# Attention projections as three products of rounded high and low parts, turned tokens in three buffers, the mask one batch at a time

## The reference

```python
src_trans = (src @ W_src.T + b_src) * mask[:, :, None]      # 256 x 512 per batch
tgt_trans = (tgt @ W_tgt.T + b_tgt) * mask[:, :, None]      # 256 x 256 per batch
k, v = split(src_trans); q = tgt_trans                      # 8 heads of 32
scores = where(mask == 0, -inf, q k^T / sqrt(32))
update = softmax(scores) @ v
x = x + tanh(g) * (concat([tgt, update]) @ W_out.T + b_out)
```

## Time and profile before

| | us |
|---|---|
| median of 3 runs | 698.89 |
| lowest, highest | 697.07, 701.77 |
| span of the profiled execution | 696.1 |
| PE busy | 657.9 (95%) |
| PE weight loads busy | 457.6 (66%) |
| ACT busy | 452.6 (65%) |
| DVE busy | 428.5 (62%) |
| POOL busy | 202.2 (29%) |

### The profile page before, as it was taken

How to read it: one execution, slowest core, us unless ns; L and a number is a source line. 1 busy time by engine, 2 the same in 40 slices (tenths; PEclk the granted TensorE clock), 3 DMA queues, 4 the chain that set the end, 5 groups by cost and what they waited for, 6 DMA issues and landing times.

```text
span 696.1 us, 11909 instructions
## 1 busy us (share of the span) xinstructions
PE 657.9 (95%) x3653; PEld 457.6 (66%) x3653; DVE 428.5 (62%) x981; ACT 452.6 (65%) x1204; POOL 202.2 (29%) x299
## 2 busy tenths in 40 slices
PE   5988899999999999699999999999999997799997
PEld 3754555554544447588888888888888875556654
DVE  7973857777765548466767566556665685343522
ACT  7766665535555534667887787788778877646452
POOL 6574424210110012124442342333223230142110
PEclk9999999999999999899999999999999999999999
DMA  8721108501000004433344443433444430001112
GB/s 269 244 96 61 62 31 257 81 1 61 1 0 1 0 1 124 101 87 99 98 113 123 123 116 84 107 93 94 119 122 122 92 80 14 2 1 61 43 49 90
DMA packets 45809, 57.90 MB, mean 83 GB/s; under 512 B 13152, under 2 KB 24258, under 8 KB 45634
## 3 DMA queue, kind: packets, MB, share of 16 engines
q1 hardware_dynamic: 45762, 57.33, 30.4%
HBM read 27.46 MB, written 4.19 MB: 45 GB/s over the span
## 4 chain that ended last, share of the span: by engine, by line
PE 79%; SPq 6%; DVE 3%; ACT 3%; DMA 3%; issue 2%; POOL 2%; DVEq 0%; POOLq 0%; ACTq 0%
PE bank L1197 12%; PE bank L1502 7%; PE bank L1414 6%; PE bank L1432 6%; PE bank L1209 6%; SPq L531 5%; PE bank L1455 5%; PE bank L1645 4%; PE bank L1478 4%; PE bank L1441 4%; PE bank L1495 4%; PE bank L1173 3%; PE bank L1635 3%; PE bank L1177 2%; PE bank L1636 2%
## 5 line engine op out<-in xcount | busy, mean ns | idle before, releaser
L976 ACT ACTIVATE c_junk<-bank,c_nmx 128x256 bf16<-128x256 f32 x256 | 116.6, 470 | 9.3 <-DVE c_nmx L1971 9.2
L1971 DVE TENSOR_REDUCE c_nmx<-bank 128x4 f32<-128x1024 f32 x64 | 75.3, 1219 | 35.7 <-PE bank L1455 35.7
L1197 PE MATMUL bank<-b_o,cw 128*128 128x512 f32 x192 | 90.6, 603 | 1.8 <-ACT b_o L831 1.8
L998 ACT ACTIVATE c_pT<-bank 128x1024 f32<-128x1024 f32 x64 | 62.0, 1017 | 7.0 <-PE bank L1478 5.9
L807 ACT ACTIVATE b_h<-bank,cb 128x512 f32<-128x512 f32 x48 | 32.9, 687 | 51.1 <-PE bank L1197 51.0
L1096 ACT ACTIVATE d_h<-bank,b_col 128x512 f32<-128x512 f32 x64 | 39.6, 686 | 39.3 <-PE bank L1636 39.3
L1197 PEld LDWEIGHTS bank<-b_o,cw 128*128 128x128 f32 x192 | 34.2, 190 | 43.4 <-issue 39.7
L1414 PE MATMUL bank<-c_ctxT,wsrcT 128*128 128x256 f32 x256 | 62.1, 388 | 0.6 <-ACT c_ctxT L957 0.6
L1432 PE MATMUL bank<-wsrcT,c_ctxT 128*128 128x256 f32 x240 | 56.7, 379 | 0.0
L1478 PE MATMUL bank<-c_stack 99*128 99x256 f32 x256 | 47.8, 320 | 7.9 <-DMA c_stack<-c_rows 7.5
L1414 PEld LDWEIGHTS bank<-c_ctxT,wsrcT 128*128 128x128 f32 x256 | 48.6, 194 | 7.2 <-ACT c_ctxT L957 0.9
(11 more groups left out here) (202 smaller groups left out, 1383.0 us busy)
## 6 DMA issues: line engine op xcount, KB each, us to landing
c_stack<-c_parts SPq DMA_DIRECT2D x192, 128.0 KB
a_ctx<-in_ctx SPq DMA_DIRECT2D x16, 512.0 KB, 4.0
c_ctx<-in_ctx SPq DMA_DIRECT2D x16, 512.0 KB, 3.3
out_x<-x_sb SPq DMA_DIRECT2D x7, 512.0 KB, 2.9
x_sb<-in_x SPq DMA_DIRECT2D x3, 1024.0 KB, 11.0
mask_b<-in_mask_BxS_fk SPq DMA_DIRECT2D x1, 2048.0 KB, 12.4
x_sb<-in_x SPq DMA_DIRECT2D x2, 512.0 KB, 5.6
wsrc_raw<-in_L_xattn_W_src SPq DMA_DIRECT2D x1, 1024.0 KB, 7.1
```

The source lines that it names most:

```text
L976: op = nc.scalar.activation(c_junk[:, tc, j, :], scores(tc)[:, j, :], ACT.Exp, bias=c_nmx[hg][:, tc, j:j + 1], accum_out=c_sum[hg][:, tc, ...
L998: nc.scalar.activation(c_pT[hg][:, :, q * S:(q + 1) * S], scores(q), ACT.Exp).then_inc(c_pT_ok, 1)
L1197: op = mm(bank[2 * u + h][:], cw1[:, c, h * P:(h + 1) * P], b_o[n % LANES][:, c, :], start=c == 0, stop=c == DK - 1)
L1971: v.tensor_reduce(c_nmx[hg][:, tc, :], scores(tc), AXIS.X, ALU.max, negate=True)\
```

## The change

Five things change. (1) Every projection of stage C becomes three float32r products, high by high, high by low and low by high, in one accumulation (in_parts, out_half). (2) For that each turned operand gets a low part: ACT's copy out of PSUM now writes the rounded high part, and DVE subtracts it from the PSUM bank (ctxL_c, xnL_c, updateL_c); PE's waits move from the copies to the low parts. The weights get theirs on POOL once (split_weights), from a full copy w_full. (3) The turned tokens are kept in three buffers (XNS), so that ACT's second copy goes; the first turn, xnT_c(0), moves into slot 11. (4) The mask is loaded per batch, 128 KB into one of two buffers (mask_in), and both uses of biased wait for it. (5) All 16 bodies are written out, without a loop. Some buffers are laid out anew in SBUF, and DVE's last xn_d(1) waits for the last token turn.

```diff
+XNS = 3
+PRODUCTS = ((0, 0), (0, 1), (1, 0))
...
-def over_batches(eng, body):
-
-    for b in range(HEAD):
-        body(b, b % 2)
-    with eng.Fori(HEAD // 2, B // 2 - 1) as i:
-        body(2 * i, 0)
-        body(2 * i + 1, 1)
-    for b in range(B - 2, B):
+def over_batches(body):
+
+    for b in range(B):
         body(b, b % 2)
...
-        mask_b = sb("mask_b", [P, B, S])
+        mask_b = [sb(f"mask_b{s}", [P, S]) for s in range(2)]
...
-        wsrcT = sb("wsrcT", [P, FK, 2 * D])
-        wtgtT = sb("wtgtT", [P, DK, D])
-        woutT = sb("woutT", [P, 2 * DK, D])
+        with ExitStack() as st:
+            w_full = sb("w_full", [P, 7, 512], F32, st)
+        wsrcT, wtgtT, woutT = zip(*([sb(f"{n}_{part}", [P, k, d], F32R)
+                                     for n, k, d in (("wsrcT", FK, 2 * D), ("wtgtT", DK, D), ("woutT", 2 * DK, D))]
+                                    for part in ("lo", "hi")))
+        wsrcT, wtgtT, woutT = wsrcT[::-1], wtgtT[::-1], woutT[::-1]
...
-            (mask_b[:], mask.partition_broadcast(P)),
...
+            def mask_in(b):
+                need(sp, c_q_ok, b - 1)
+                need(sp, c_k_ok, b - 1)
+                sp.dma_start(mask_b[b % 2][:], row_on_all(mask[b])).then_inc(c_mask_in[b % 2], 16)
+
+            mask_in(0)
+            mask_in(1)
...
                     masks_c(b + 1, 1 - b % 2)
+                if b + 2 < B:
+                    mask_in(b + 2)
                 if b + 3 < B:
                     stream_c(b + 3, 1 - b % 2)
...
+            def split_weights(t):
+                pool.wait_ge(s_wT, t + 1)
+                high, low = turned_rows(t)
+                nc.gpsimd.tensor_copy(high, w_full[:, t, :]).then_inc(s_wsplit, 1)
+                pool.wait_ge(s_wsplit, 2 * t + 1)
+                nc.gpsimd.tensor_tensor(low, w_full[:, t, :], high.bitcast(F32), ALU.subtract).then_inc(s_wsplit, 1)
+
+            for t in range(WT_BANKS):
+                split_weights(t)
...
-            def xnTq_c(b, src=5):
+            def xnT_c(b, src=5):
                 need(act, c_xnT_ps, b + 1)
-                need(act, c_q_ps, b)
-                need(act, c_xnT_ok, b)
-                nc.scalar.copy(c_xnTq[:].rearrange("p c t -> p (c t)"), bank[src][:]).then_inc(c_xnTq_ok, 1)
-
-            def xnT_c(b, s):
-                need(act, c_xnTq_ok, b + 1)
-                need(act, c_out_ps, b - 1)
-                nc.scalar.copy(c_xnT[s][:], c_xnTq[:]).then_inc(c_xnT_ok, 1)
+                need(act, c_out_ps, b - XNS + 1)
+                nc.scalar.copy(c_xnT[b % XNS][0][:].rearrange("p c t -> p (c t)"), bank[src][:]).then_inc(c_xnT_ok, 1)
...
-                xnT_c(b + 1, 1 - s)
                 if ahead:
-                    xnTq_c(b + 2)
+                    xnT_c(b + 2)
                 update_c(b, s, 0)
...
+            def in_parts(dst, still, moving):
+
+                chunks = len(still[0])
+                for i, (a, b) in enumerate(PRODUCTS):
+                    for f in range(chunks):
+                        op = mm(dst, still[a][f], moving[b][f], start=i == 0 and f == 0,
+                                stop=i == len(PRODUCTS) - 1 and f == chunks - 1)
+                return op
...
             def k_c(b, s, dst=4, parts=range(DK)):
-                need(pe, c_ctxT_ok, 2 * b + 2)
+                need(pe, c_ctxL_ok, 2 * b + 2)
+                turned = [[c[s][:, f, :] for f in range(FK)] for c in (c_ctxT, c_ctxL)]
                 for m in parts:
-                    for f in range(FK):
-                        op = mm(bank[dst][:, m * S:(m + 1) * S], wsrcT[:, f, m * P:(m + 1) * P],
-                                c_ctxT[s][:, f, :], start=f == 0, stop=f == FK - 1)
+                    weights = [[w[:, f, m * P:(m + 1) * P] for f in range(FK)] for w in wsrcT]
+                    op = in_parts(bank[dst][:, m * S:(m + 1) * S], weights, turned)
...
                 need(pe, c_xn_ok, b + 1)
-                need(pe, c_ctxT_ok, 2 * b + 1)
+                need(pe, c_ctxL_ok, 2 * b + 1)
...
             def q_c(b, s, dst=5):
-                need(pe, c_xnTq_ok, b + 1)
+                need(pe, c_xnL_ok, b + 1)
                 for m in range(DK):
-                    for c in range(DK):
-                        op = mm(bank[dst][:, m * S:(m + 1) * S], wtgtT[:, c, m * P:(m + 1) * P],
-                                c_xnTq[:, c, :], start=c == 0, stop=c == DK - 1)
+                    weights = [[w[:, c, m * P:(m + 1) * P] for c in range(DK)] for w in wtgtT]
+                    op = in_parts(bank[dst][:, m * S:(m + 1) * S], weights,
+                                  [[x[:, c, :] for c in range(DK)] for x in c_xnT[b % XNS]])
...
-                need(pe, c_up_ok, n - 1 if is_last(b, B) else n)
+                need(pe, c_upL_ok, n - 1 if is_last(b, B) else n)
...
-            def out_part(s, k, f):
-                src = c_xnT[s][:, f, :] if f < DK else c_upT[s][:, f - DK, :]
-                return mm(bank[7][:, k * D:(k + 1) * D], src[:, k * P:(k + 1) * P], woutT[:, f, :],
-                          start=f == 0, stop=f == 2 * DK - 1)
+            def out_half(b, s, k, h):
+
+                held = (c_xnT[b % XNS], (c_upT[s], c_upL[s]))[h]
+                dst = bank[7][:, k * D:(k + 1) * D]
+                for i, (p, q) in enumerate(PRODUCTS):
+                    for f in range(DK):
+                        op = mm(dst, held[p][:, f, k * P:(k + 1) * P], woutT[q][:, h * DK + f, :],
+                                start=h == 0 and i == 0 and f == 0,
+                                stop=h == 1 and i == len(PRODUCTS) - 1 and f == DK - 1)
+                return op
             def out_begin(b, s, k=0):
                 if k == 0:
-                    need(pe, c_xnT_ok, b + 1)
                     need(pe, c_x3, b)
-                for f in range(DK):
-                    out_part(s, k, f)
+                out_half(b, s, k, 0)
             def out_c(b, s, begun=(0,)):
-                need(pe, c_up_ok, 2 * b + 2)
+                need(pe, c_upL_ok, 2 * b + 2)
                 for k in range(TS):
-                    for f in range(DK if k in begun else 0, 2 * DK):
-                        op = out_part(s, k, f)
+                    if k not in begun:
+                        out_half(b, s, k, 0)
+                    op = out_half(b, s, k, 1)
...
             ctxT_c(0, 0, 1, 5)
             ctxT_c(0, 0, 0, 7)
-            xnT_c(0, 0, 6)
             slot_b(PAIRS - 1)
-            pe.wait_ge(c_ctxT_ok, 2)
+            pe.wait_ge(s_wsplit, 2 * WT_BANKS)
+            pe.wait_ge(c_ctxL_ok, 2)
             q_c(0, 0, 7)
             k_c(0, 0, 6)
             slot_b(PAIRS)
-            for k in range(TS):
-                for f in range(FK):
-                    op = mm(bank[3][:, k * D:(k + 1) * D], c_ctxT[0][:, f, k * P:(k + 1) * P],
-                            wsrcT[:, f, D:2 * D], start=f == 0, stop=f == FK - 1)
-            op.then_inc(c_v_ps, 1)
+            v_c(0, 0, 0, 3)
+            v_c(0, 0, 1, 3)
...
+                need(dve, c_mask_in[b % 2], 16 * (b // 2 + 1))
                 need(dve, ps, b + 1)
                 need(dve, used, use_count)
                 for m in range(DK):
                     op = v.scalar_tensor_tensor(dst[:, m, :], src_bank[:, m * S:(m + 1) * S], col[:, m:m + 1],
-                                                mask_b[:, bass.ds(b, 1), :].rearrange("p o t -> p (o t)"),
-                                                ALU.add, ALU.mult)
+                                                mask_b[b % 2][:], ALU.add, ALU.mult)
                 op.then_inc(ok, 1)
+
+            def ctxL_c(b, s, h, src=4):
+                need(dve, c_ctxT_ok, 2 * b + 2 - h)
+                need(dve, c_v_ps, b - 1)
+                v.tensor_tensor(c_ctxL[s][:, 2 * h:2 * h + 2, :].rearrange("p c t -> p (c t)"), bank[src + h][:],
+                                c_ctxT[s][:, 2 * h:2 * h + 2, :].rearrange("p c t -> p (c t)").bitcast(F32),
+                                ALU.subtract).then_inc(c_ctxL_ok, 1)
+
+            def xnL_c(b, src=5):
+                high, low = (part[:].rearrange("p c t -> p (c t)") for part in c_xnT[b % XNS])
+                need(dve, c_xnT_ok, b + 1)
+                v.tensor_tensor(low, bank[src][:], high.bitcast(F32), ALU.subtract).then_inc(c_xnL_ok, 1)
+
+            def updateL_c(b, s, hg):
+                need(dve, c_up_ok, 2 * b + hg + 1)
+                need(dve, c_out_ps, b - 1)
+                v.tensor_tensor(c_upL[s][:, hg, :], bank[6][:, hg * S:(hg + 1) * S],
+                                c_upT[s][:, hg, :].bitcast(F32), ALU.subtract).then_inc(c_upL_ok, 1)
...
             def last_c(b, s):
+                updateL_c(b - 1, 1 - s, 0)
                 maxima_c(b, s, 0)
                 xnT_d(1, 1)
                 xnT_d(1, 0)
                 shift_c(b, 0)
+                updateL_c(b - 1, 1 - s, 1)
                 maxima_c(b, s, 1)
                 finish_c(b - 1, 1 - s)
                 shift_c(b, 1)
```

(27 more changed lines are left out.)

83 lines of the change are left out of this document (50 added, 33 removed).

## The result

The changed kernel takes **739.9 us** (median of 4 runs, 735.9 to 742.7) against 698.0 for the kernel before on the same chip (4 runs, 696.1 to 701.8): 1.0587 times as long over all runs, with an interval of 1.054 to 1.063. The forecast was 708, with a range of 690 to 718. The direction was right, the size was not. The profiled execution has a span of 740.7 us against 696.1; it was the longest of the four (742.7, 2.7 above their median).

The account below looks back on a forecast made before the run. Relieved of PE's bound, the kernel was to be held by the loop through DVE and ACT with a late mask: +4.5, +2.7, +1.3, -0.5, +0.8 make +8.8, span 704.9, plus 2.8 for the median, 708 us; range 690 to 718.

Parts of the forecast that it names:

- PE's 95%: PE's busy share of the span before; PE may lose 2 us a batch, the kernel collect only 0.5.
- The loop lead + 18.5 through DVE and ACT: Per batch: lead, from first scores to first maxima, plus 18.5 us; 19.3 with the old 0.82, against PE's 19.84.
- The mask is the step that decides: DVE waits for the per-batch mask before the key's bias; lead 1.85 instead of 0.94, period 20.35 us.
- The low parts ahead of the second maxima: updateL_c and ctxL_c on DVE ahead of the second maxima_c: cost nothing, ending when it starts anyway, about 9.7 us in.
- rival "mask in time": The loop through DVE and ACT binds: 13 x 19.45 = 252.9 us, kernel 693 to 696; chance 0.22.
- The loop through SP: Stack DMAs and mask row issued one by one, row landing 2.19 us later: lead + 17.8 = 18.6 a batch.
- m: Start of the mask row's issue to the mask's landing: 2.75 us taken, ends 2.19 and 4.0; next lead is m - 0.90.
- 4.5: Batches 1 to 13: one period of 19.45 and twelve of 20.35, 263.7 against 259.2 us, so +4.5.
- rival "fetches and a late mask together": m near 4.0 and a fetch hit in most bodies, periods of 21.6 and more, 720 or above; chance 0.12.
- +1.3: Stage start: PE waits for xnL_c(0) before q_c(0), so q_c with k_c end at 261.2 instead of 259.8 us.
- +2.7: Instruction fetches with 13 bodies written out: three late landings at 0.9 us each.
- updateL_c adds what out_c saves: Body 15 and behind it: the update's low part costs what the output saves, so 0 us from last scores to end.

Follow-up runs that it names:

- experiment 1: Changed kernel with each batch's mask sent for one batch earlier, nothing else moved: 698.8 us, 1.001 of the kernel before.
- experiment 7: Changed kernel, mask still late, with 18 unused products on PE between the first scores and the next rows: 735.4 us, 1.0537 of the kernel before.
- experiment 12: Changed kernel with the mask's transfer reading 128 different context rows of 1 KB instead of one mask row (masking left out): 715.4 us.
- experiment 11: Changed kernel, late mask, with the context load of batch b+3 moved from right behind the mask to behind rows_c(b - 1, 1): 725.5 us.
- experiment 9: experiment 8 plus 5 and 8 unused PE products around the first half's update in the last batch: 688.5 us, 0.987 of the kernel before.
- experiment 8: experiment 1 plus two of DVE's low parts moved ahead of the previous block's updates at the stage's start: 692.6 us, 0.994 of the kernel before.
- Experiment 4: The kernel before with its loop over the batches written out, nothing else: 697.9 us, 1.001 of the kernel before.
- experiment 5: Changed kernel, late mask, without DVE's low parts of tokens, context and update (all three products take high parts): 712.1 us, 1.020 of the kernel before.
- experiment 2: Changed kernel, mask still late, with the key's bias on DVE moved behind the next batch's first maxima: 731.8 us.

## Why the prediction was wrong

**Right.** PE's 95% were not the price list: PE has lost work and the kernel got slower. A product takes 0.12 us (four in 0.48 at 501.70). The loop lead + 18.5 through DVE and ACT, which had only 0.5 us to give, is the loop that binds. The mask is the step that decides, DVE waits for it at `biased(c_kT)` and PE for the low part at `rows_c`, as it was written. The low parts ahead of the second maxima are hidden: DVE's second maxima start 9.3 behind the first (468.22 against 458.87 in experiment 1). The 13 periods of 252.9 us of the rival "mask in time" are 254.8 in experiment 1, where the mask is in time by construction. The loop through SP was priced too low: the mask row's 2.19 was one landing at the start, and in experiment 1 the first scores stand 2.45 to 4.04 behind the start of the row's issue, which with five waits of PE for that row gives the periods above 19.45.

**Wrong, the term that was mis-sized: m, the time from the start of the mask row's issue to the landing of the mask.** The prediction let the mask land 2.75 us behind the start of the row's issue and held 4.0 for the upper end. It is 4.55 in the batch shown, 4.7 on average. Put into the prediction's own formula, m - 0.90 gives a lead of 3.8 (measured 3.57) and a period of 22.3 instead of 20.35. The 13 periods grew by 33.0 us where 4.5 stood for the mask, 28.5 too little. Twelve batches in which m is 1.95 longer are 23.4 of these, and the lead that came out 0.23 shorter takes 2.8 away. The 0.56 by which a period exceeds its lead + 18.5, which experiment 7 puts down to the clock, adds 6.7, and the first of the 13 periods, counted without a mask wait, was 20.7 instead of 19.45 (1.2): 28.5. The error came from sizing a transfer by its bytes between a lone 16 KB load and a lone 512 KB load. Neither has the two things that this one has, a single source row for 128 partitions (1.6 us, experiment 12) and a 512 KB transfer issued 0.42 us behind it (0.8, experiment 11). The upper end was "nor later than the context load that today has its place", as if that load, standing ahead of its successor, bounded one of another shape. The Trainium skill's 2 µs a transfer (SBUF — State Buffer, "The DMA setup-cost knee") with its m of 3.08 was nearer, and short of it as well; with rows of its own and the context beside it the mask took 2.2, which agrees.

The rival "fetches and a late mask together" had named m near 4.0, periods of 21.6 and more and 720 or above, with a chance of 0.12. It had the time and the late mask right and the reason wrong: seven of twelve masks had no fetch beside them and landed after 3.6 to 4.0 us all the same.

**Missed: the clock.** The prediction named half clock in body 0 from rows 1 (0.86) and yet gave PE new waits at no cost in clock. It is about 0.7 us a batch (experiment 7: 22.63 to 21.95), 8 us in the trace, 4.5 between medians, and 2.4 at the end of the stage (in the trace of experiment 9 against that of 8).

**Missed: the second wait at the start.** +1.3 had followed q_c(0) only. The low part of batch 1's context got no line of its own: it stands behind `update_b(11, 1)` on DVE, k_c(1) waits 4.01 us for it, and at half clock. Moving it and xnL_c(0) forward gave 6.4 us of the start back (280.4 to 274.0, experiment 8).

**Probably too much: the fetches.** +2.7 was taken from two late landings beside a fetch. Experiment 4, with the same bodies written out, shows no difference: a fetch starts there 0.7 us behind the mask row's issue in the same two batches (rows at 413.7 and 433.8), and their periods are 19.85 and 19.84. So the fetch was not enough to make the two periods long. The rule of the Trainium skill that calls such a crossing mostly hidden (Runtime: NRT & Kernel Launch, "Instruction fetch mechanics") agrees with that run. But experiment 4 has no late mask, on which the term rested. In the changed kernel five masks with a fetch beside them landed 0.2 later than the others on average, 1 us in all; in experiment 12 it was 0.7, 3.3 us in all.

**The end.** "updateL_c adds what out_c saves" covers the two waits of 0.95 and misses what went with them: PE stood more between short pieces of work, and its clock fell for 10 us (4.1 us in all, most of it given back in experiment 9).

## What to carry to other kernels

When a load that was made once becomes one per iteration, find who waits for it and what is queued behind that wait, and ask for the transfer a whole iteration ahead: here the place in SyncE's list was worth 41 us, and everything else that could be had 10. Price a transfer by one of the same pattern and with the same neighbours, not by its bytes, and when the trace has none, widen the upper end. Where TensorE gets new waits of 1 to 4 us, count its clock behind them too; and once a bound engine has been relieved, the gain is what the next loop has to spare, half a microsecond of the two that PE lost per batch in this case.

## What the runs showed of the hardware

- 128 KB into 128 partitions took 3.8 us from one DRAM row of 1 KB that all partitions read, 2.2 from 128 rows of 1 KB, at the same place in the same list, with a 512 KB load issued 0.42 us behind both (medians of experiment 12 and the changed kernel). Without that load behind it the single row took 3.0 (experiment 11).
- TensorE's granted clock fell to half for 3.4 us at or behind nine of eleven waits of 2.0 to 3.1 us, in batches in which it was busy 85%; with 18 products of 0.12 us put into each wait it stayed at full speed from 302 to 629 us (experiment 7). In experiment 5, where its waits between 300 and 600 us were no longer than 1.5, it stayed at full speed too. In the last batch waits of 0.4 to 1.1 us in a row went ahead of a drop of 6.8 us (experiments 1 and 8), and with 13 such products there was none (experiment 9).
- VectorE instructions of 8 columns took 1.15 us instead of 0.17 when they met a GpSimd sum or difference of 512 columns, and ended with it (experiment 2; one of them in each batch of every other kernel as well, 1.04 at 464.38 in experiment 1).
